# A vision tower on one core: latent attention's output projection one tile per step, TensorE's order regrouped, and the embedding's next loads issued by GpSimd

## What is computed

```python
h = (x - mu) * rsqrt(var + eps) * ln_scale + ln_bias     # x: (32, 37, 256)
c_q, c_kv = h @ w_down_q.T, h @ w_down_kv.T              # 128 latents each
q, k, v = heads(c_q @ w_up_q.T), heads(c_kv @ w_up_k.T), heads(c_kv @ w_up_v.T)   # 16 heads of 64
q, k = rope(q), rope(k)
attn = softmax(q @ k.T / 8)
out = (attn @ v) @ w_out.T + x
x = layernorm(x + out)                                   # so z = 2 x + projection
```

## Time and profile before

| | us |
|---|---|
| median of 3 runs | 1123.51 |
| the lowest and highest of them | 1122.18, 4631.71 |
| the profiled execution | 1126.98 |
| its span, first to last instruction | 1125.2 |
| TensorE busy in the span | 926.1 |
| VectorE, ScalarE, GpSimd busy | 605.5, 525.5, 329.4 |
| mean granted TensorE clock | 0.874 |

### The profile page before, as it was taken

One profiled execution on the slowest core, in us unless ns is written; L12 is line 12 of the kernel. 1 busy time (PEld: TensorE's weight loads), 2 busy tenths in 40 slices (PEclk: granted clock), 3 DMA queues, 4 the chain that ended last, 5 costly groups with the idle time before them and its releaser, 6 DMA issues. The chain is left out here.

```text
span 1125.2 us, 26130 instructions
## 1 busy us (share of the span) xinstructions
PE 926.1 (82%) x10336; PEld 684.7 (61%) x10336; DVE 605.5 (54%) x1301; ACT 525.5 (47%) x940; POOL 329.4 (29%) x419
## 2 busy tenths in 40 slices
PE   4889958389999799768995499999479999988664
PEld 4878735267777557557884244445367778777332
DVE  3566746556666379745663433323554554532385
ACT  2354638376656289635441255552123333522354
POOL 0202320545543100030331334441453544531101
PEclk9999968699999889879996699999589999966685
DMA  5300020200000100001004952224200000000001
GB/s 182 113 3 2 3 108 11 80 1 2 1 0 1 43 3 1 0 11 39 3 3 138 404 164 40 47 38 99 82 2 3 2 3 3 3 2 2 1 1 43
DMA packets 24466, 47.40 MB, mean 42 GB/s; under 512 B 4664, under 2 KB 16115, under 8 KB 23714
## 3 DMA queue, kind: packets, MB, share of 16 engines
q1 hardware_dynamic: 19524, 39.09, 10.0%
q0 software_dynamic: 3936, 5.51, 3.0%
q10 hardware_dynamic: 894, 1.23, 0.3%
HBM read 38.35 MB, written 7.47 MB: 41 GB/s over the span
## 5 line engine op out<-in xcount | busy, mean ns | idle before, releaser
L2719 PE MATMUL psum<-L2f_EW,weights_even 128*64 x176 | 81.6, 607 | 1.8 <-ACT weights_even L2418 1.3
L2720 PE MATMUL psum<-L2f_W,weights_even 128*64 128x512 f32 x176 | 81.6, 607 | 0.0
L2379 POOL DMA_INDIRECT expert_sums<-weights_even,L2f_target x20 | 35.0, 1750 | 77.5 <-DVE weights_even L2601 54.1
L1048 PE MATMUL psum<-L_cT,weights_odd 128*128 128x222 f32 (+1 forms) x192 | 49.4, 392 | 9.4 <-DVE L_by_sin L937 8.3
L2614 DVE TENSOR_TENSOR weights_even<-psum,weights_even 128x512 f32<-128x512 f32 x22 | 15.2, 692 | 73.4 <-PE psum L2720 71.3
L2235 PE MATMUL psum<-weights_even,L1f_H 128*111 128x256 f32 x176 | 47.4, 428 | 7.4 <-DVE L1f_H L2166 7.4
L937 DVE TENSOR_TENSOR L_by_cos<-psum,vectors_odd 128x444 f32<-128x444 f32 (+1 forms) x48 | 26.6, 554 | 49.9 <-PE psum L1048 49.4
L2426 ACT ACTIVATE L2f_W<-L2f_EW 128x1024 f32 x44 | 46.3, 1053 | 13.7 <-DMA L2f_EW<-experts 7.5
L876 ACT ACTIVATE L_PT<-psum 101x296 f32<-101x296 f32 x32 | 13.3, 416 | 83.7 <-PE psum L1089 83.1
L2719 PEld LDWEIGHTS psum<-L2f_EW,weights_even 128*64 128x64 f32 x176 | 22.7, 139 | 44.5 <-issue 44.5
L419 ACT ACTIVATE L_PT<-psum 101x296 f32<-101x296 f32 x64 | 26.9, 421 | 48.2 <-PE psum L615 48.1
(11 more groups left out here) (452 smaller groups left out, 2665.2 us busy)
## 6 DMA issues: line engine op xcount, KB each, us to landing
L2f_EW<-experts SPq DMA_DIRECT2D x24, 512.0 KB, 13.0
weights_even<-L_w SPq DMA_DIRECT2D x4, 1024.0 KB
patch_ring<-patches SPq DMA_DIRECT2D x11, 333.0 KB, 5.1
expert_sums<-L_blank SPq DMA_DIRECT2D x1, 1184.0 KB
out<-X SPq DMA_DIRECT2D x10, 111.0 KB
weights_odd<-L_wo SPq DMA_DIRECT2D x1, 1024.0 KB
expert_rows<-X SPq DMA_DIRECT2D x1, 960.0 KB
expert_sums<-X SPq DMA_DIRECT2D x1, 960.0 KB
```

What stands on the lines that cost most here:

```text
L1048: mm = nc.tensor.matmul(bank[:, h * NC2:h * NC2 + width(u)], wu[:, (2 * g + h) * 128:(2 * g + h + 1) * 128], cT[:, u % 2, n // 4, 0:width( ...
L2379: nc.gpsimd.indirect_dma_start(sums[:, :], bass.IndirectOffsetOnAxis(ap=target[:, j:j + 1], axis=0), Y[:, j % 2, :], None, compute_op=ALU. ...
L2719: nc.tensor.matmul(core.bank(bank)[PAIR[0], :], xsT[:, j % 2, c, PAIR[0]], own, start=c == 0, stop=c == KD - 1)
L2720: mm = nc.tensor.matmul(core.bank(bank)[PAIR[1], :], xsT[:, j % 2, c, PAIR[1]], cols(W1[:, part], KD, NF)[:, c], start=c == 0, stop=c == K ...
```

## The change

In latent attention the output projection goes one tile at a time, tiles 0 to 9 at the steps that `TILE_AT` names and tile 10 at the end: in k = 1 between the second transpose and the second `up`, in the other steps (and at s = 16) between the two gathers. It writes columns 0 to 255 of bank M2 alone. VectorE's `residual` takes one tile, in k = 0 and 1 ahead of the remaining turns, in k = 2 behind them. TensorE's order puts the two halves of the scores directly behind each other and the `up`s beside the transposes or, later, beside a gather or at the step's end; `naturals` always stands between the two halves of `values`. VectorE does `shift` ahead of the first turn. ScalarE does `exps` right behind the first copy of transposed probabilities, ahead of the copies that follow. GpSimd's `norm` moves from k = 1 to k = 2. In the embedding the next stage's seven loads move from ScalarE's queue to GpSimd's, behind VectorE's first low part.

```diff
@@ embed
             def _(pool):
...
+                pool.wait_ge(low, 1)
+                load_next(pool, next_loads, next_sem)
...
-                    if t == RING - 1:
-                        load_next(act, next_loads, next_sem)
@@ latent_attention
+        TILE_AT = {4: 0, 5: 1, 7: 2, 8: 3, 10: 4, 11: 5, 13: 6, 14: 7, 15: 8, 16: 9}
+
+        def projected(s):
+            return sum(at <= s for at in TILE_AT)
+
+        def pairs_for(t):
+            return min((PER * t + PER - 1) // 2, NP - 1) + 1
@@ GpSimd
-                    if k == 1 and u >= 1:
+                    if k == 2 and u >= 1:
                         norm(u - 1)
+                norm(NU - 2)
                 norm(NU - 1)
@@ ScalarE
+                    if s >= 1:
+                        p_T(s - 1, 0)
+                    if s < NP:
+                        exps(s)
                     if k == 2 and u + 2 < NU:
                         x_T(u + 2)
                     if s >= 1:
-                        p_T(s - 1, 0)
-                    if k == 0 and s + 3 < NP:
-                        nat_out(s + 3)
+                        p_T(s - 1, 1)
...
@@ VectorE
+                def residual(t):
+                    u, m = t // 2, t % 2
+                    p = u % 2
+                    dve.wait_ge(y_ps, t + 1)
                     after(dve, norm_done, u - 1)
+                    nc.vector.scalar_tensor_tensor(z[:R, p, m], X[:R, t, :], 2.0, core.bank(M2)[:R, 0:D], ALU.mult, ALU.add).then_inc(z_done, 1)
...
+                    if s < NP:
+                        shift(s)
                     for n in todo[:1]:
                         turn(*n)
                     if s < NP:
-                        shift(s)
                         sums(s)
-                    if k == 1 and u >= 1:
-                        residual(u - 1)
+                    if s in TILE_AT and k != 2:
+                        residual(TILE_AT[s])
                     for n in todo[1:]:
                         turn(*n)
+                    if s in TILE_AT and k == 2:
+                        residual(TILE_AT[s])
@@ TensorE
+                def o_project(t, s):
+                    u, k = unit_of(s), s % 3
+                    pe.wait_ge(oT_done, 2 * pairs_for(t))
+                    pe.wait_ge(nat_done, min(s + 3, NP))
+                    if k == 2 and u + 2 < NU:
+                        pe.wait_ge(c_done, u + 3)
+                    after(pe, z_done, t)
+                    first = min(PER * t, B - PER) % RING * T
+                    for c in range(8):
+                        mm = nc.tensor.matmul(core.bank(M2)[:R, 0:D], OT[:, c, first:first + R], wo[:, c, :], start=c == 0, stop=c == 7)
                     mm.then_inc(y_ps, 1)
```

More of the change, by code:

```diff
@@ L881, in o_T @@
                     act.wait_ge(o_ps, 2 * s + half + 1)
-                    after(act, y_ps, (2 * s - RING) // IMGS + 1)
+                    after(act, y_ps, (2 * s + 1 - RING) // PER + 1)
                     nc.scalar.activation(OT[:, 4 * half:4 * half + 4, at:at + 2 * T], cols(core.bank(M3)[:, 0:8 * T], 4, 2 * T), ACT.Copy).then_inc(oT_done, 1)
@@ L908, in _ @@
                         o_T(s - 1, 0)
-                    if k != 0 and s + 3 < NP:
+                    if s + 3 < NP:
                         nat_out(s + 3)
@@ L1014, in _ @@
                 maximum_of_x(core, core.maxima[:R, 0:1], 0, AHEAD_L3)
-                residual(NU - 1)
+                residual(NT - 1)
             @block.tensor
@@ L1057, in naturals @@
                         pe.wait_ge(c_done, u + 2)
-                    if k == 1:
-                        after(pe, z_done, u - 1)
+                    after(pe, z_done, projected(s - 3))
                     for b in range(2):
@@ L1112, in values @@
                     mm.then_inc(o_ps, 1)
-                def o_project(u):
-                    pe.wait_ge(oT_done, 2 * pairs_of(u + 1))
-                    pe.wait_ge(nat_done, min(3 * u + 7, NP))
-                    after(pe, z_done, u)
-                    for m, t in enumerate(UNITS[u][1]):
-                        first = min(PER * t, B - PER) % RING * T
-                        for c in range(8):
-                            mm = nc.tensor.matmul(core.bank(M2)[:R, m * D:(m + 1) * D], OT[:, c, first:first + R], wo[:, c, :],
-                                                  start=c == 0, stop=c == 7)
+                def o_project(t, s):
[8 more added lines that the diff above has]
+                        mm = nc.tensor.matmul(core.bank(M2)[:R, 0:D], OT[:, c, first:first + R], wo[:, c, :], start=c == 0, stop=c == 7)
                     mm.then_inc(y_ps, 1)
@@ L1154, in _ @@
                         score(s, 0)
-                    if k == 2 and u + 2 < NU:
-                        x_T(u + 2)
+                        score(s, 1)
                     if s == NP:
@@ L1159, in _ @@
                         weights_T(2)
+                    if s >= 1:
+                        p_T(s - 1, 0)
                     if todo:
                         up(*todo[0])
-                    if s < NP:
-                        score(s, 1)
+                    if k == 2 and u + 2 < NU:
+                        x_T(u + 2)
                     if s >= 1:
-                        p_T(s - 1, 0)
-                    if k == 0 and s + 3 < NP:
-                        naturals(s + 3)
-                    if k == 1 and u >= 1:
-                        o_project(u - 1)
+                        p_T(s - 1, 1)
+                    if s in TILE_AT and k == 1 and s < NP:
+                        o_project(TILE_AT[s], s)
+                    late = todo[1:] if k == 0 else todo[2:]
+                    if k != 0 and todo:
+                        up(*todo[1])
                     if k == 2 and u + 2 < NU:
@@ L1172, in _ @@
                     if s >= 1:
-                        p_T(s - 1, 1)
                         gather(s - 1, 0)
-                    if todo:
-                        up(*todo[1])
+                    if s in TILE_AT and (k != 1 or s == NP):
+                        o_project(TILE_AT[s], s)
+                    if late:
+                        up(*late[0])
                     if s >= 1:
@@ L1184, in _ @@
                         weights_T(4)
-                    if k != 0 and s + 3 < NP:
+                    if s + 3 < NP:
                         naturals(s + 3)
-                    if len(todo) > 2:
-                        up(*todo[2])
                     if s >= 1:
                         values(s - 1, 1)
+                    if len(late) > 1:
+                        up(*late[1])
                     if s == NP - 1:
                         weights_T(0)
-                o_project(NU - 1)
+                o_project(NT - 1, NP)
         st.clear()
```

18 lines of the change are left out of this document (4 added, 14 removed).

## The result

The kernel after takes 1115.8 us in the median of six runs (1112.1 to 1120.3) against 1126.7 for the kernel before on the same chip: a ratio of 0.9912, with the interval 0.9886 to 0.9938, some 10 us. A second set gave 0.9863, 0.9829 to 0.9898, some 15 us. The forecast was 19.4 us. The ratios leave out the one run of the kernel before that took 4631.7 us and the runs, two of s_apart and one of best1, that were over 1.5% slower than the fastest of their kernel. The profiled execution took 1114.3 us (before 1127.0).

The account below looks back on a forecast made before the run. TensorE bounds the regular steps, with half clock in the latent stage's first and last steps. Terms -5.0 + 0 + 1.5 - 4.5 - 11.4 = -19.4 took the profiled 1126.98 to 1107.6, less 3.5 to the median: 1104 us, range 1089 to 1119.

Parts of the forecast that it names:

- no change beyond 2%: Whole kernel: a measured time within 2% of the kernel before, given a chance of 0.59.
- The last steps, -11.4: Step 12 to tile 10's end: spread projection blocks keep TensorE's clock up and cover waits; -11.4 us, bounds -18 and 0.
- the clock would fall in each of four stretches: Last steps: the clock falls between projection blocks for 4 to 5 us each time, giving back 6 us of the gain.
- Steps 0 and 1, -4.5: Latent stage's start: shift first shortens step 0's idle time and spares step 1 half clock; -4.5 us, bounds -1 and -6.4.
- The embedding, -5.0: Embedding: ScalarE's load issues, TensorE's idle time and half-speed tile go, less a later identity; -5.0 us, bounds -7.3 and -2.4.
- I take 2.3 us lost, between the ends: Embedding: GpSimd's earlier loads delay the identity, by nothing up to 3.2 us; 2.3 us taken as lost.
- The rule on DMA queues: Embedding: engines alternate between queues by whole packets, so the identity waits for about half the new load's work; -5.7 us.
- Steps 2 to 11, +1.5: Regular latent steps: 0 for three units plus 1.5 us for feeding TensorE's queue.
- I add 1.5: Scores: two halves in a row take matmuls without rest, lengthening issue gaps; +1.5 us, bounds -1.5 and +8.
- 0 for the units: Regular steps: shape, wait, turn and projection terms summed to +0.5 a unit, a list count gave -0.3; 0 taken for three.
- The rival of scores that starve the queue: Scores back to back: +8 us in place of +1.5, whole kernel 1110.6 us; chance 0.12.
- The slower rival: Regular steps: grouped narrow matmuls lower the clock, +67 us if all at half speed; some 1140 us, chance 0.06.

Follow-up runs that it names:

- s_apart: Kernel after with TensorE's first `up` of a step moved back between the two score halves; 1129.8 us, ratio 1.0033.
- best1: Kernel before with single-tile projection, embedding loads on GpSimd gated on tables and identity, and after's order for step 0 alone; 1101.2 us, ratio 0.9754.
- p_blocks: Kernel after with projection tiles 6 and 7 together at step 13, 8 and 9 together at step 16; 1125.0 us, ratio 1.0000.
- t_only: Kernel before with only the single-tile projection and residual and GpSimd's norm at k = 2, other orders and embedding as before; 1112.9 us, ratio 0.9895.
- t_late: Kernel before with the single-tile part and embedding loads on GpSimd gated on tables and identity, no regrouping; 1105.3 us, ratio 0.9824.
- best2: Kernel before with single-tile projection, embedding loads on GpSimd gated on tables and identity, and after's order for steps 0 and 1; 1103.3 us, ratio 0.9783.
- a_again: Kernel after run once more, unchanged; 1109.9 us, ratio 0.9863.
- e_late: Kernel after with GpSimd issuing the embedding's seven loads only once the tables and identity have landed; 1106.8 us, ratio 0.9840.
- e_undo: Kernel after with the embedding's seven loads back on ScalarE's queue; 1116.4 us, ratio 0.9917.
- g_only: Kernel after with all projection in two-tile blocks again, at steps 4, 7, 10, 13, 16: the regrouping without the tiles; 1133.3 us, ratio 1.0037.
- r_mid: Kernel after with VectorE's residual in k = 1 moved behind the first of the two remaining turns; 1108.2 us, ratio 0.9857.
- s_pt: Kernel after with the first four transposes of the step before placed between the two score halves; 1115.0 us, ratio 0.9926.

## Why the prediction was right or wrong

**Direction, no change beyond 2%, and mechanism of the largest term: right.** The forecast was no change beyond 2% and a gain, and so it came; but 19.4 us were forecast and 10 measured (15 in the second set). 1104 lies below both sets' medians, and 1116 is inside the range.

**The last steps, -11.4: right.** Measured -13.0, and +0.6 behind tile 10. p_blocks shows the cause, a clock of 0.61 against 0.90 in the same 35 us. The step held that the clock would fall in each of four stretches; in after it fell in two, and in t_only in none. Luck has a part in that: t_only's longest issue gap there was 0.81 us, while t_late, best1 and best2, with the same order there, each had one of 1.07 or 1.08 and a fall behind it.

**Steps 0 and 1, -4.5: right in this execution (-6.2), though it holds in only half of the executions.** The idle time fell from 3.78 to 1.92 and 0.33 us, as worked out. But the same order left the clock at full speed in only some executions: of eight profiles with after's order there, four (after, a_again, e_late, p_blocks) took 18.7 us, and four (e_undo, best2, g_only, r_mid) 21.4 to 23.1. In e_undo, whose latent stage is after's to the letter, the stretch stood at

```profile
830.50:853.50 23.00, 19.01 (x370) 15.28 (x368) 11.65 (x20) 6.32 (x11) 12.21 (x18) 0.78 0.01 2
```

So the term has a spread of 4 us that the order of the instructions doesn't account for. Part of it is there before step 0. In the four of 18.7 us the start of the stage took 19.7 to 19.8 us, with the clock up again 13.6 to 14.0 us before the first score; in e_undo, g_only and r_mid it took 22.1 to 22.5, with the clock up 10.8 to 11.2 before it. The instructions are the same. It isn't all, since best2 started as fast (19.7) and took 23.0. So the latent column of after, a_again, e_late and p_blocks holds some 5 to 7 us of good luck in these two stretches.

**The embedding, -5.0: wrong, -0.4.** The mechanism was right and its size was off. The step "I take 2.3 us lost, between the ends" is what failed: the loss was 6.9 us in after and 5.3 to 6.4 in three more of the seven ungated profiles, and -0.6 to 1.5 in the other three. In the lost ones the identity went from 14.47 to between 18.3 and 19.2, 3.8 to 4.7 us, beyond the 3.2 us that the prediction gave as its upper end from the bytes alone. With the idle time of 6 us before tile 2 the clock also fell, which stood in the prediction only as a bound. That it is one or the other from execution to execution was in no rival. The rule on DMA queues, in the page "DMA: Bandwidth & Descriptors" of the Trainium skill (section "Queues, rings and completion order"), would have had the engines take turns and given -5.7. One of the seven profiles agrees (g_only, the cast at 15.93 and a stage of 39.0 us, -5.8); the others lie at -0.4 to -2 or at -7.5 and -7.9.

**Steps 2 to 11, +1.5: wrong, +7.0.** The parts, from the rows above: turn waits 6.3 in place of 3.0, +3.3; gaps 3.7 in place of 1.4, +2.3; half clock behind each of the three gaps, 3.4 us x 0.35, +3.6; the second half's wait and the copy between the gathers, 1.4 in place of 0.7, +0.7. That is 9.9, and the difference to 7.0 is put down to what the grouping saved in changes of shape: an estimate of -2.9 against the -1.3 x 3.3 = -4.3 forecast. No run prices that saving by itself. The turn waits were in the working almost to size (0.55, 0.85 and 0.8 forecast per unit; 0.45, 0.8 to 1.0 and 0.98 measured). What failed is the step "I add 1.5" for feeding the queue: the gaps were counted as idle time, and the clock behind them was not. The 1.5 came out as 2.3 of gaps and 3.6 of half clock, 5.9. The rival of scores that starve the queue named the place and had a chance of 0.12; its +8 was close to the +7.0, though it put all of it on the gaps and carried the embedding's -5. The prediction also took 0 for the units, where its own list of terms said +0.5 each and the rest of the parts came to 1.1.

**The slower rival** (the grouping lowers the clock in the regular steps) had the mechanism right and the size wrong: three falls in ten steps, not a third of the stretch. g_only and s_apart, where less covers the waits, reach ratios of 1.004 and 1.003.

## What to carry to other kernels

Small dense blocks spread over steps of narrow work do more for TensorE's clock than the same work in fewer, larger blocks; here that was 10 to 17 of the 76 us. When instructions are regrouped, list for each one that moves what it was covering (a copy, a turn, a queue's refill), for the saving per change of shape was some 0.1 us (an estimate from the earlier trace rows) and a lost cover costs up to 0.6 and may cost the clock. Two blocks of many small matmuls behind each other are a risk where an instruction fetch falls into them, so look for the fetches in the trace before they are put together. One profile of a kernel isn't enough to price a stage here: from the start of the latent stage to step 2 the same instructions took up to 7 us more in some executions than in others. A transfer moved to an idle queue should be gated on whatever critical transfers it would race with.

## What the runs showed of the hardware

- In steps 2 to 11 a gap of 1.07 to 1.71 us inside the scores, with full work on both sides, was followed by some 3.4 us at 1.2 GHz in 11 of 13 cases with the halves in a row; one of up to 0.87 us with a piece between never was, in 17. Waits of 0.8 to 1.0 us for a turn had no fall behind them, those of 2.05 to 2.09 (g_only) had one in three of three, those of 1.16 to 1.37 (s_apart, s_pt) in two of eight.
- The gaps end 2.25 to 2.94 us after the start of a 16 KB instruction fetch, in 41 of 41 cases. In the 14 gaps of after's latent order the fetch had started 0.2 to 0.9 us into the two score halves; that was so at no steps but 3, 8 and 9 of steps 2 to 11.
- Loads issued by GpSimd while SyncE's tables were in flight delayed the last of these by 3.8 to 4.7 us in four of seven profiled executions, by 1.5 in one and not at all in two. In three of the four the identity was issued as early as without them.
- The first four pieces of the latent stage (16 matmuls), ahead of step 0 and the same in both kernels, took 5.92 us in the profile of before and 3.30 in that of after. TensorE's granted clock there is a matter of the execution.
